# Dealing row maxima two to an attention step, with turns, bias and outputs on top

## The reference, cut to what matters

```python
attn = softmax(einsum('bhqd,bhkd->bhqk', q, k) * scale, axis=-1)
attn = attn + rel_bias            # added after the softmax
out  = einsum('bhqk,bhkd->bhqd', attn, v)
```

## Time and profile before

| | |
|---|---|
| runs | 675.83, 675.56, 673.68 us; median 675.56 us |
| profiled execution, its own time | 676.92 us |
| its span, first to last instruction | 675.1 us |
| TensorE, VectorE, ScalarE, GpSimd busy | 607.4 us, 518.8 us, 378.9 us, 114.2 us |
| mean granted TensorE clock | 0.981 of full speed |
| the chain that ended last, by engine | TensorE 64%, VectorE 22%, ScalarE 6% |

### The profile page before, as it was taken

The page is one execution under the profiler, slowest core; times in us unless marked ns, Lnnn a source line. Parts: engine busy times, 40 slices in busy tenths (PEclk is TensorE's granted clock), DMA queues, the critical chain, the costliest instruction groups (busy, mean ns, idle before and its releaser), DMA issues.

```text
span 675.1 us, 9217 instructions
## 1 busy us (share of the span) xinstructions
PE 607.4 (90%) x3304; PEld 240.3 (36%) x3304; DVE 518.8 (77%) x930; ACT 378.9 (56%) x692; POOL 114.2 (17%) x140
## 2 busy tenths in 40 slices
PE   7878799999989698899999998999999988887897
PEld 5344545644457262222222221222222213234443
DVE  5657767854759987997997989999999994429634
ACT  3935123323500206786887877888888888862231
POOL 5941021100104550103012000000000021001000
PEclk9979899999989889999999999999999999999999
DMA  7100000000211221201201010010000000000001
GB/s 228 54 1 0 1 0 1 0 1 0 90 57 58 93 65 32 88 1 53 66 14 44 2 32 26 2 55 2 29 28 2 2 2 1 0 1 0 4 29 31
DMA packets 18989, 20.22 MB, mean 30 GB/s; under 512 B 3968, under 2 KB 12672, under 8 KB 18944
## 3 DMA queue, kind: packets, MB, share of 16 engines
q1 hardware_dynamic: 17040, 18.78, 8.9%
q0 software_dynamic: 656, 0.59, 0.3%
q10 hardware_dynamic: 1248, 0.27, 0.2%
HBM read 15.23 MB, written 4.19 MB: 29 GB/s over the span
## 4 chain that ended last, share of the span: by engine, by line
PE 64%; DVE 22%; ACT 6%; issue 2%; DVEq 2%; DMA 1%; SPq 1%; POOL 1%; POOLq 0%; ACTq 0%
PE banks L1545 18%; PE banks L1531 13%; DVE negmax L1121 8%; PE banks L1464 7%; PE banks L1257 7%; PE banks L1335 4%; ACT arena L818 3%; PE banks L1378 3%; PE banks L1326 2%; PE banks L1270 2%; DVE arena L975 2%; PE banks L1588 1%; DVE arena L1028 1%; PE banks L1479 1%; PE banks L1492 1%
## 5 line engine op out<-in xcount | busy, mean ns | idle before, releaser
L1121 DVE TENSOR_REDUCE negmax<-banks 128x2 f32<-128x1024 f32 x256 | 301.6, 1221 | 26.1 <-PE banks L1464 22.8
L818 ACT ACTIVATE arena<-banks 128x512 f32<-128x512 f32 x512 | 268.4, 603 | 90.3 <-PE banks L1531 89.4
L1531 PE MATMUL banks<-arena 59*128 59x512 bf16 x512 | 150.9, 382 | 10.8 <-ACT arena L818 9.4
L1464 PE MATMUL banks<-arena 56*128 56x512 bf16 x512 | 121.4, 390 | 22.4 <-DVE negmax L1121 19.1
L1545 PE MATMUL banks<-arena 128*32 128x512 f32 x1024 | 136.4, 605 | 0.7 <-ACT arena L818 0.7
L1531 PEld LDWEIGHTS banks<-arena 59*128 59x128 bf16 x512 | 38.2, 94 | 160.9 <-ACT arena L818 145.9
L540 POOL TENSOR_TENSOR rstd<-veps,neghalf 128x4 f32<-128x4 f32 (+1 forms) x24 | 27.1, 1129 | 207.2 <-DVE veps L889 161.3
L1335 PE MATMUL banks<-arena,bT 128*128 128x512 f32 x128 | 60.1, 593 | 1.6 <-ACT arena L661 1.6
L661 ACT ACTIVATE arena<-banks 128x512 f32<-128x512 f32 (+1 forms) x56 | 32.1, 595 | 50.5 <-PE banks L1257 20.3
L1464 PEld LDWEIGHTS banks<-arena 56*128 56x128 bf16 x512 | 26.0, 93 | 72.0 <-DVE negmax L1121 64.4
L975 DVE TENSOR_SCALAR arena<-banks,bi 128x512 f32<-128x512 f32 x32 | 23.9, 746 | 33.0 <-PE banks L1335 33.0
(11 more groups left out here) (148 smaller groups left out, 647.3 us busy)
## 6 DMA issues: line engine op xcount, KB each, us to landing
arena<-qk_scratch SPq DMA_DIRECT2D x128, 48.0 KB
arena<-in_tab SPq DMA_DIRECT2D x4, 1024.0 KB, 6.5
qk_scratch<-arena SPq DMA_DIRECT2D x8, 384.0 KB, 2.6
arena<-qk_scratch SPq DMA_DIRECT2D x64, 16.0 KB
out<-x SPq DMA_DIRECT2D x4, 256.0 KB, 2.3
x<-in_x POOLq DMA_DIRECT2D x1, 512.0 KB, 8.4
arena<-nm_part SPq DMA_DIRECT2D x32, 4.0 KB, 1.8
x<-in_x ACTq DMA_DIRECT2D x1, 256.0 KB, 3.9
```

Source lines behind the costliest of these rows:

```text
L818: act.activation(probs[s % 2][:, h, :], score_bank(g, n), ACT.Exp, scale=SCALE).then_inc(exp_done, 1)
L1121: return dve.tensor_reduce(negmax[:, buf, keys, :, at_tile], slot, axis=AXX, op=ALU.max, negate=True)
L1464: last = pe.matmul(slot[:, side, :], qs[rows, buf, pair, t * P:(t + 1) * P], ks[rows, buf, pair, keys * HALF:(keys + 1) * HALF], start=Tru ...
L1531: pe.matmul(score_bank(g, n), ks[rows, g % BUFS, pair, t * P:(t + 1) * P], qs[rows, g % BUFS, pair, q * HALF:(q + 1) * HALF], start=True, ...
```

## The change

The function `beside` says which ring items belong to step j. Before, it cuts the list of a round's items into 16 shares by position, so that each kind of item counts as one. After, an item goes to the step given by the number of maxima ahead of it in the list, two maxima to a step; other items fall to the step whose next maximum they stand before, and the output goes to the last step. In `RING`, the bias is also moved one maximum later.

```diff
-RING = NEXT_MAXES[:4] + [("bias", 0, 0), NEXT_MAXES[4], ("bias_turn", 0, 0)] + NEXT_MAXES[5:] + AFTER_NEXT + [("out", 0, 0)]
+RING = NEXT_MAXES[:5] + [("bias", 0, 0), NEXT_MAXES[5], ("bias_turn", 0, 0)] + NEXT_MAXES[6:] + AFTER_NEXT + [("out", 0, 0)]
...
             def beside(items, j):
-                whole = RING_PLAIN if items is RING_BEFORE_LAST else items
-                share = whole[j * len(whole) // STEPS:(j + 1) * len(whole) // STEPS]
-                return [items.index(x) for x in share if x in items]
+                steps, maxes = [[] for _ in range(STEPS)], 0
+                for k, item in enumerate(items):
+                    steps[STEPS - 1 if item[0] == "out" else maxes * STEPS // MAXES].append(k)
+                    maxes += item[0] == "max"
+                return steps[j]
```

## The result

The changed kernel took 679.12 us (median of 5 runs, 678.48 to 679.93) against 675.83 before: 1.0056 of the time, 95% interval [1.0036, 1.0077]. Forecast were 673.8 us and a range up to 676.0. It is slower, and the time lies outside the range.

What follows compares the result with a forecast made beforehand. Neither engine was full; a dependence ring (weigh, score 3, ScalarE's exponential, score 2) set 2.39 us a step. Biased rounds -0.80, plain -1.16, round before the last +0.20: -1.76 from median 675.56 gives 673.8 us, range 671.4 to 676.0.

Steps and rivals of the forecast that it cites:

- Step 7 without its third maximum: With two maxima in step 7, step 8 finds its slot free: 2.39 us, 1.06 us less in each such round.
- The biased rounds: Four rounds: 1.06 gained at step 8, 0.86 lost by step 4; each 0.20 us shorter, 0.80 in all.
- the start of the bias turn on the fresh copy: Step 3 of biased rounds: TensorE starts the bias turn 0.15 us after VectorE's copy of the bias ends.
- forecast wait of 0.44: Step 3 of biased rounds: a new TensorE wait of 0.44 us for the copy, ahead of the bias turn.
- The plain rounds: Two rounds: -1.06 at step 8, +0.48 for the turn's new place; -0.58 us each, -1.16 in all, to 40.4 us.
- the turn's 0.65: Plain rounds: the turn costs 0.65 us ahead of the weigh of step 12, no longer 0.17 ahead of step 11.
- The round before the last: Step 8 gives 1.06, but joining starts at 550.03 against 549.83, so the round ends 0.20 us later.
- The clock is 1.00, so nothing is to be had from it.: Opening reading of a biased round: the clock is at 1.00 and offers no gain.
- the hidden wait: Rival, chance 0.20: bias turn in biased rounds starts at 315.53 or nearly, without the new wait; sum -3.5, 672.0 us.
- VectorE as the bound: Rival, chance 0.08: a maximum moved into VectorE's gaps gives back its whole time; sum -5.9, 669.6 us.
- the copy behind a maximum: Rival, chance 0.05: in biased rounds the copy waits for a whole maximum, 1.24 us; sum +3.2, 678.8 us.
- the stall that stays: Rival, chance 0.05: step 8's stall has another origin than step 7's third maximum and remains; +5.7, 681.3 us.

Runs made afterwards that it cites:

- e9: The changed kernel plus 3 unused TensorE products ahead of the turn of the round before the last; 673.94 us, ratio 0.9986.
- e3: The kernel before, with the new `beside` in the round before the last alone; 676.31 us, ratio 1.0011.
- e4: The changed kernel run again with nothing altered, 12 runs; 677.99 us, ratio 1.0022 to the kernel before.
- e10: The changed kernel, idle ahead of the turn left, 3 unused products before score 2 in steps 12 to 14 of the round before the last; 675.30 us, ratio 1.0015.

## Why the prediction was wrong

**Step 7 without its third maximum** was right: 2.39 in place of 3.45 wherever it was looked for, and no wait at step 8.

**The biased rounds** were right to 0.05 us: 0.25 gained on average against 0.20. The mis-sized term is the start of the bias turn on the fresh copy. I took 0.15 us from the turn's row; it started 315.24 - 314.50 - 0.69 = 0.05 behind the copy, and the interval into step 3 is 5.40 for 5.48. (The 0.28 us in its row does not compare with the forecast wait of 0.44: the row counts from the modelled end of the score, the forecast from the earliest start.) Two of the three rounds gained 0.30, one only 0.14: its last two steps took 0.17 longer, from a cause that was not looked for.

**The plain rounds** were right: 40.41 against 40.4, with the turn's 0.65 moved to step 12.

**The round before the last** is where it failed, in the words "The turn and the weigh of step 11 follow at fixed distances, so this round ends 0.20 us later." These words and the +0.20 in the sum put the clock at nothing. The distances held up to that weigh: 548.36 - 544.54 = 3.82 against 2.56 before, so 1.26 lost where 1.06 had been gained, the 0.20 of the forecast. Behind it they did not hold. The layout moved two short waits of TensorE (0.89 at step 8 and 0.44 ahead of the turn) into one of 1.47, and I priced that as time alone. Behind it the clock halved for 13.6 us and took 4.77 us. The sum then reads -2.33 + 4.77 = +2.44, which is the difference of the two spans, 677.5 - 675.1 = 2.4. It includes the 0.32 us by which this execution was ahead from the start.

The idle could have been worked out. By the forecast the turn starts 550.03 + 0.19 + 0.15 - 547.07 = 3.30 us behind the weigh of step 10, and in the trace before, the last scores behind a step with two maxima end 546.97 + 0.59 - 545.74 = 1.82 us behind its weigh (step 9), which leaves 1.48 us without work.

The step that let this through stands at the start: "The clock is 1.00, so nothing is to be had from it." That was read in one biased round, in which the longest wait of TensorE for VectorE is 0.89 us. It says what the clock does now, not what it will do when a wait grows. The mean of 0.981 over the whole kernel before was a sign that it does fall here: in its trace it stands at 0.88 from 200 to 240 us, ahead of these rounds. No rival had a clock in it. The Trainium skill, page "TensorE: Matmul & The Clock Gate", section "Why this matters for your kernels", warns that idle gaps between bursts of matrix products put the clock back. The trace agrees as far as the row with 1.47 us of idle is the last wait for VectorE ahead of the fall; the gaps that the page names are longer, and here the measurement decides. I had used that page for the order of products and not for this.

Of the rivals, the hidden wait, VectorE as the bound, the copy behind a maximum and the stall that stays were each refuted by the rows of steps 2 to 8. Two of them ended on the slower side, where the result lies, but by mechanisms that are not there; that the copy's rival, at 678.8, is 0.3 us from the measured time is chance.

## What to carry to other kernels

When a change moves waits on TensorE, write down the longest single idle that results, not only the sum of idle time: here waits of 0.89 and 0.44 us kept the clock, and one of 1.47 often did not. A long idle is a place to look and not yet a price, since others as long were followed by no fall (below). Look first at the stretches with the least work around them; here that was the one round in which no further work fills the steps behind the wait, though no run tells whether that had a part in the fall. Take several executions before a clock is called safe. A handful of products with unused results, placed in a wait that exists anyway, cost nothing where it was shorter than the wait (3.81 us from weigh to weigh in e9 against 3.82), and is a quick test of whether a clock is the cause.

## What the runs showed of the hardware that was not expected

- All four profiled executions with an idle of 1.47 or 1.48 us ahead of the turn (the changed kernel, e3, e4, e10) show the granted clock at 0.50 from 1 to 2 us behind it. By times and mean clocks it was 13 of 17 executions of the changed kernel, but only two clear cases of 12 in e3, with the same idle and the same steps around it. Idles of 0.89 us at steps 4 and 8, and of 0.44 and 0.61 ahead of the turn, were followed by no fall in these profiles.
- The length of an idle does not decide by itself. In the changed kernel's trace TensorE was idle for 1.56 us up to 138.58 and for 2.99 us up to 618.33, outside the attention, and the clock is 1.00 behind both; in e4's trace it is at 0.50 behind the second. Why e3 fell less often is open: it ran on another chip, and its idle came later in the profiled execution (549.41 against 547.84), but profiled falls stand behind turns from 546.00 to 549.41.
- TensorE's first transpose of a fresh VectorE result started 0.05 us behind its end for the copy of the bias (128x512, row at 315.24), against 0.15 for the joined maxima (128x32). What makes the difference is not shown.
- Half the clock did not double the steps: they took 3.70 us against 2.39. A weigh took 1.93 us in place of 1.06, while TensorE's wait for ScalarE ahead of score 2 went from 0.47 to 0.26 us; score 2 and the weigh still wait for ScalarE.
